# A fused transformer with a routed last layer: when the third slot's weights are loaded, how the experts are chosen, and where two norms stand

## The reference, cut to what matters

```python
x = x + _L0_xattn_ref(16, 64, 256, w, u, _layernorm(x), ctx)        # wkv, the first stage
...
x = x + _L2_ffn_ref(_layernorm(x), w_gate_up, w_proj)               # the ternary stage
x = x + _L3_xattn_ref(_layernorm(x), ctx, ctx)
x = x + _L3_ffn_ref(_layernorm(x), gate_w, w1, w2, w3)              # the experts:
    router_logits = x @ gate_w.T                                    # 1024 x 8
    probs = softmax(router_logits)
    top_w, top_i = top_k(probs, 2)
    top_w = top_w / sum(top_w)
    for e in range(8):
        h = silu(x @ w1[e].T) * (x @ w3[e].T)                       # 256 -> 896
        out = out + w_dense[:, e:e + 1] * (h @ w2[e].T)             # 896 -> 256
```

## Time and profile before

| | us |
|---|---|
| median of 3 runs | 753.79 (752.92 to 754.49) |
| the profiled execution | 752.44 |
| its span, first to last instruction | 750.7 |
| TensorE busy | 607.6 (81%) |
| VectorE busy | 463.6 (62%) |
| ScalarE busy | 304.8 (41%) |
| GpSimd busy | 235.4 (31%) |

### The profile page before, as it was taken

One profiled execution on the slowest core, in us unless ns is written; L12 is line 12 of the kernel. 1 busy time (PEld: TensorE's weight loads), 2 busy tenths in 40 slices (PEclk: granted clock), 3 DMA queues, 4 the chain that ended last, 5 costly groups with the idle time before them and its releaser, 6 DMA issues.

```text
span 750.7 us, 12278 instructions
## 1 busy us (share of the span) xinstructions
PE 607.6 (81%) x4701; PEld 458.9 (61%) x4701; DVE 463.6 (62%) x963; ACT 304.8 (41%) x512; POOL 235.4 (31%) x250
## 2 busy tenths in 40 slices
PE   1551999958841699999696998886999999999993
PEld 1241556736731255566443666546999999999993
DVE  6998688897889898997856777965111111111110
ACT  4920255436664158878643566611111111111110
POOL 3312065346401798620511312001122222222211
PEclk9875799989985589999997999989899999999998
DMA  8000502200025427550303000118599999899942
GB/s 281 0 0 0 183 5 69 68 4 2 2 47 127 100 56 182 159 137 31 114 1 148 1 1 1 56 59 338 204 316 321 324 310 323 302 330 320 314 138 70
DMA packets 39594, 102.14 MB, mean 136 GB/s; under 512 B 6648, under 2 KB 31096, under 8 KB 35256
## 3 DMA queue, kind: packets, MB, share of 16 engines
q1 hardware_dynamic: 29312, 89.69, 35.2%
q0 software_dynamic: 4368, 5.90, 3.9%
q10 hardware_dynamic: 5856, 5.77, 2.2%
HBM read 87.45 MB, written 14.55 MB: 136 GB/s over the span
## 4 chain that ended last, share of the span: by engine, by line
PE 56%; DVE 30%; issue 5%; ACT 3%; DMA 2%; POOL 2%; POOLq 0%; DVEq 0%; SPq 0%; ACTq 0%
PE bank L1935 19%; PE bank L1948 9%; PE bank L1497 5%; DVE region L1225 3%; PE bank L1098 3%; PE bank L1138 3%; PE bank L580 2%; DVE XN L375 2%; PE bank L1122 2%; PE bank L1517 2%; PE bank L514 2%; DVE region L2227 2%; PE bank L2058 2%; DVE region L784 1%; PE bank L2065 1%
## 5 line engine op out<-in xcount | busy, mean ns | idle before, releaser
L1935 PEld LDWEIGHTS bank<-wide,region 128*128 128x128 f32 x1288 | 149.4, 194 | 2.7 <-ACT wide L1852 1.6
L1935 PE MATMUL bank<-wide,region 128*128 128x128 f32 x1288 | 150.0, 277 | 1.0 <-ACT wide L1852 1.0
L1818 DVE TENSOR_TENSOR wide<-wide,bank 128x512 f32<-128x512 f32 (+1 forms) x46 | 28.6, 621 | 130.6 <-ACT wide L1862 130.6
L1862 ACT ACTIVATE wide<-bank 128x512 f32<-128x512 f32 (+1 forms) x46 | 25.0, 544 | 183.8 <-PE bank L1935 183.8
L1225 DVE TENSOR_REDUCE region<-bank 128x2 f32<-128x512 f32 x128 | 80.1, 680 | 6.9 <-PE bank L1098 6.3
L1948 PE MATMUL bank<-region,wide 128*128 128x256 f32 x322 | 73.4, 379 | 0.7 <-DVE wide L1829 0.7
L1161 ACT ACTIVATE region<-bank 128x1024 f32<-128x1024 f32 x64 | 62.9, 1024 | 15.7 <-PE bank L1122 15.5
L1702 POOL DMA_INDIRECT residual_rows<-wide,to_row x23 | 36.4, 1581 | 100.0 <-DMA residual_rows<-wide,to_row 77.3
L1948 PEld LDWEIGHTS bank<-region,wide 128*128 128x128 f32 x322 | 59.4, 190 | 8.2 <-issue 1.0
L1098 PE MATMUL bank<-region 128*128 128x256 bf16 x256 | 52.0, 305 | 8.9 <-DVE region L1225 5.8
L389 POOL TENSOR_TENSOR rstd<-vareps,half_neg 128x4 f32<-128x4 f32 x16 | 18.3, 1146 | 123.9 <-DVE vareps L385 123.9
(11 more groups left out here) (311 smaller groups left out, 1138.0 us busy)
## 6 DMA issues: line engine op xcount, KB each, us to landing
region<-in_L_ffn_experts_dram SPq DMA_DIRECT2D x23, 1792.0 KB, 9.6
region<-in_L_ffn_experts_dram SPq DMA_DIRECT2D x23, 896.0 KB, 4.8
region<-ctx_parts SPq DMA_DIRECT2D x24, 192.0 KB
region<-norm_parts SPq DMA_DIRECT2D x24, 192.0 KB
channel_values<-wide ACTq DMA_DIRECT2D x8, 512.0 KB, 4.4
ctx_parts<-region SPq DMA_DIRECT2D x40, 64.0 KB, 2.0
region<-in_L_ffn_w_gate_up_dram SPq DMA_DIRECT2D x4, 512.0 KB, 5.4
wide<-channel_values SPq DMA_DIRECT2D x16, 128.0 KB, 2.6
```

The source lines that it names most:

```text
L1818: e.tensor_tensor(HB8[par][:, cols], silu8[:, cols], bank[hf][:, 512:512 + P * (hi - lo)], ALU.mult)\
L1935: last = e.matmul(bank[hf][:, at_:at_ + P], w[:, col:col + P], xbT[par][:, P * c:P * c + P], start=(c == 0), stop=(c == KC - 1))
```

## The change

Six things change. (1) SP waits for slot 1's gathered rows before it loads slot 2's weights. (2) The two experts are chosen by the shifted logits, without the exponent; the probabilities and the weights of the two are made later, behind the row marks. (3) Slot 0's tokens are marked by their rank within expert 0 straight from the counts, ahead of the positions; the counts move to another bank, and fewer unused matmuls run. (4) `from_row` comes before `to_row`, and an unused lane gathers row 0, where it gathered the row with its own lane's number. (5) The lane weights' matmuls stand ahead of slot 2's transposes. `lo_hot` moves to another place in memory, and ScalarE and GpSimd each wait once for row numbers. (6) In the first stage the norm of tiles 0 to 3 stands behind GpSimd's loop; in the ternary stage the variance and normalisation of tiles 4 to 7 both come at step 1, behind the rest-of-rest subtraction.

```diff
             def second_half(t):
                 if t < 2:
                     vec_invert(e, 6 + t)
+
+            def rest_half(t):
                 if t == 1:
                     e.wait_ge(x_done, 5 * NT)
                     norm_variance(e, ch, 5, 4, NT)
-                if t == 2:
                     norm_tiles(e, 5, 4, NT)
...
-            tile_steps([(hidden, 0), (mean_square, 1), (rest, 1), (second_half, 0), (add, 2), (rest_of_rest, 1)], next_norm)
+            tile_steps([(hidden, 0), (mean_square, 1), (rest, 1), (second_half, 0), (add, 2), (rest_of_rest, 1), (rest_half, 0)], next_norm)
...
                 x8 = e.value_load(etab[0:1, s:s + 1], min_val=0, max_val=E8 - 1)
+                if s == 2:
+                    e.wait_ge(s_moe["rows_in1"], 16)
                 weights_in(e, s, L3_ffn_experts[bass.ds(x8, 1)].rearrange("x p w -> (x p) w"))
...
                     if s >= 1:
                         e.wait_ge(s_moe["hidden_ready"], 2 * s + hf - 1)
+                    elif hf == 1:
+                        e.wait_ge(s_moe["rows_known"], 1)
...
+            ch.link(e.iota(lane_below, [[1, P]], base=-N, channel_multiplier=0, allow_small_or_imprecise_dtypes=True))
...
-            e.wait_ge(s_moe["logits_exp"], 1)
-            ch.link(e.tensor_reduce(v["z"], r["ex"], AX.X, ALU.add))
-            ch.link(e.reciprocal(v["rz"], v["z"]))
-            ch.link(e.tensor_tensor(r["pr"], r["ex"], per_tile(v["rz"]), ALU.mult))
-            for src, m, o in (("pr", "m1", "o1"), ("p2", "m2", "o2")):
+            e.wait_ge(s_moe["logits_shifted"], 1)
+            for src, o in (("lg", "o1"), ("p2", "o2")):
+                if o == "o2":
...
+                else:
+                    ch.link(e.scalar_tensor_tensor(r["key"], r["lg"], 0.0, per_expert(rev8), ALU.is_equal, ALU.mult))
...
+            ch.link(e.tensor_tensor(nearest, ps(5, 0, NT), r["cnt"][:, 0, :], ALU.add))
+            ch.link(e.scalar_tensor_tensor(nearest, cnt_b[:, 0:NT], -float(N), nearest, ALU.mult, ALU.add))
+            for hf in range(2):
+                e.tensor_tensor(first_hot[:, 4 * hf:4 * hf + 4, :], lane_below.unsqueeze(1).broadcast_to([P, 4, P]),
+                                nearest[:, 4 * hf:4 * hf + 4].unsqueeze(2).broadcast_to([P, 4, P]), ALU.is_equal)\
+                    .then_inc(s_moe["first_marked"], 1)
...
-            ch.link(e.tensor_tensor(nearest, posk[:, 0, :], posk[:, 1, :], ALU.min))
-            for hf in range(2):
-                e.tensor_tensor(first_hot[:, 4 * hf:4 * hf + 4, :], lane_no.unsqueeze(1).broadcast_to([P, 4, P]),
-                                nearest[:, 4 * hf:4 * hf + 4].unsqueeze(2).broadcast_to([P, 4, P]), ALU.is_equal)\
-                    .then_inc(s_moe["first_marked"], 1)
...
-            e.wait_ge(s_moe["routing_made"], 3)
-            ch.link(e.tensor_copy(spare, ps(5, SLOTS, 2 * SLOTS)))
-            ch.link(e.scalar_tensor_tensor(source, ps(5, 0, SLOTS), -1.0, spare, ALU.add, ALU.add))
-            ch.link(e.scalar_tensor_tensor(spare, source, 0.0, spare_row, ALU.is_lt, ALU.mult))
-            ch.link(e.tensor_tensor(to_row[:, :], source, spare, ALU.add))
-            e.tensor_scalar(from_row[:, :], to_row[:, :], N - 1, None, ALU.bitwise_and).then_inc(s_moe["rows_known"], 1)
-
+            e.wait_ge(s_moe["logits_exp"], 1)
+            ch.link(e.tensor_reduce(v["z"], r["ex"], AX.X, ALU.add))
+            ch.link(e.reciprocal(v["rz"], v["z"]))
+            ch.link(e.tensor_tensor(r["pr"], r["ex"], per_tile(v["rz"]), ALU.mult))
+            for o, m in (("o1", "m1"), ("o2", "m2")):
+                ch.link(e.tensor_tensor(r["m"], r["pr"], r[o], ALU.mult))
+                ch.link(e.tensor_reduce(v[m], r["m"], AX.X, ALU.add))
             ch.link(e.tensor_tensor(v["den"], v["m1"], v["m2"], ALU.add))
             ch.link(e.reciprocal(v["den"], v["den"]))
             e.tensor_tensor(weight8[:, 0, :], v["m1"], v["den"], ALU.mult)
             ch.link(e.tensor_tensor(weight8[:, 1, :], v["m2"], v["den"], ALU.mult))
+
+            e.wait_ge(s_moe["routing_made"], 3)
+            ch.link(e.tensor_copy(spare, ps(5, SLOTS, 2 * SLOTS)))
+            ch.link(e.scalar_tensor_tensor(source, ps(5, 0, SLOTS), -1.0, spare, ALU.add, ALU.add))
+            e.tensor_scalar(from_row[:, :], source, 0.0, None, ALU.max).then_inc(s_moe["rows_known"], 1)
+            ch.link(e.scalar_tensor_tensor(spare, source, 0.0, spare_row, ALU.is_lt, ALU.mult))
+            e.tensor_tensor(to_row[:, :], source, spare, ALU.add).then_inc(s_moe["rows_known"], 1)
...
-            busy(4, 9)
+            busy(4, 5)
             e.wait_ge(s_moe["choices_made"], 1)
...
-            busy(4, 10)
+            busy(4, 3)
...
-                if s == 1:
+                if s == 2:
                     lane_weights()
...
                 e.tensor_tensor(EV[c][:, cols], E[c][:, cols], CT[:, c, cols], ALU.mult).then_inc(s_ev, 1)
-                if u == 2:
-                    pool_norm(e, 1, 0, 4)
+            pool_norm(e, 1, 0, 4)
             pool_norm(e, 1, 4, NT)
```

More of the change, by code:

```diff
@@ L306, in program @@
         chosen_at = small(2 * NT, E8)
-        rc = {n: small(NT) for n in ("mx", "z", "rz", "m1", "m2", "k", "den", "n", "nt", "end", "base", "least", "ones")}
+        rc = {n: small(NT) for n in ("mx", "z", "rz", "m1", "m2", "k", "den", "second", "nt", "end", "base", "least", "ones")}
         cnt_b = small(NT * E8 // 2).bitcast(BF16)
@@ L328, in program @@
         BLOCKS = ((0, 4), (4, I8 // P))
-        lo_hot = small(NT * P).bitcast(BF16).rearrange("p (j l) -> p j l", l=P)
         hi_hot = small(2 * NT * 2 * SLOTS // 2).bitcast(BF16).rearrange("p (j v s) -> p j v s", v=2, s=SLOTS)
@@ L334, in program @@
         weight_rest = carve(2, NT)
+        lo_hot = carve(2 * NT, P, dt=BF16)
         weight_part = [carve(2, NT, dt=BF16) for _ in range(3)]
-        lane_no, slot_no, tile_row = small(P), small(SLOTS), small(2 * NT)
+        lane_no, slot_no, tile_row, lane_below = small(P), small(SLOTS), small(2 * NT), small(P)
         slot_of, lane_of, posk = small(2, NT), small(2, NT), small(2, NT)
@@ L1698, in store @@
                 if s == 0:
+                    e.wait_ge(s_moe["rows_known"], 2)
                     e.wait_ge(s_moe["residual_stored"], 32)
@@ L1727, in vec_experts @@
             e.tensor_tensor(r["lg"], lg, per_tile(v["mx"]), ALU.subtract).then_inc(s_moe["logits_shifted"], 1)
-            e.wait_ge(s_moe["logits_exp"], 1)
-            ch.link(e.tensor_reduce(v["z"], r["ex"], AX.X, ALU.add))
-            ch.link(e.reciprocal(v["rz"], v["z"]))
-            ch.link(e.tensor_tensor(r["pr"], r["ex"], per_tile(v["rz"]), ALU.mult))
-            for src, m, o in (("pr", "m1", "o1"), ("p2", "m2", "o2")):
-                ch.link(e.tensor_reduce(v[m], r[src], AX.X, ALU.max))
-                ch.link(e.tensor_tensor(r["m"], r[src], per_tile(v[m]), ALU.is_equal))
-                ch.link(e.tensor_tensor(r["key"], r["m"], per_expert(rev8), ALU.mult))
+            e.wait_ge(s_moe["logits_shifted"], 1)
+            for src, o in (("lg", "o1"), ("p2", "o2")):
+                if o == "o2":
+                    ch.link(e.tensor_reduce(v["second"], r[src], AX.X, ALU.max))
+                    ch.link(e.tensor_tensor(r["m"], r[src], per_tile(v["second"]), ALU.is_equal))
+                    ch.link(e.tensor_tensor(r["key"], r["m"], per_expert(rev8), ALU.mult))
+                else:
+                    ch.link(e.scalar_tensor_tensor(r["key"], r["lg"], 0.0, per_expert(rev8), ALU.is_equal, ALU.mult))
                 ch.link(e.tensor_reduce(v["k"], r["key"], AX.X, ALU.max))
@@ L1739, in vec_experts @@
                 if o == "o1":
-                    ch.link(e.scalar_tensor_tensor(r["p2"], r["o1"], -2.0, r["pr"], ALU.mult, ALU.add))
+                    ch.link(e.scalar_tensor_tensor(r["p2"], r["o1"], NEG, r["lg"], ALU.mult, ALU.add))
             e.tensor_tensor(cnt_b.rearrange("p (e t) -> p t e", e=E8), r["o1"], r["o2"], ALU.add).then_inc(s_moe["choices_made"], 1)
@@ L1751, in vec_experts @@
             ch.link(e.tensor_tensor(v["base"], v["end"], v["nt"], ALU.subtract))
-            ch.link(e.tensor_tensor(r["pos"], ps(6, 0, 64).rearrange("p (e t) -> p t e", e=E8),
+            ch.link(e.tensor_tensor(r["pos"], ps(5, 0, 64).rearrange("p (e t) -> p t e", e=E8),
                                     r["cnt"].rearrange("p e t -> p t e"), ALU.add))
@@ L1885, in pe_experts @@
             last.then_inc(s_moe["routing_made"], 1)
-            busy(4, 9)
+            busy(4, 5)
             e.wait_ge(s_moe["choices_made"], 1)
-            e.matmul(ps(6, 0, 64), before, cnt_b, start=True, stop=True)
-            e.matmul(ps(6, 64, 128), onesb, cnt_b, start=True, stop=True).then_inc(s_moe["routing_made"], 1)
-            busy(4, 10)
+            e.matmul(ps(5, 0, 64), before, cnt_b, start=True, stop=True)
+            e.matmul(ps(5, 64, 128), onesb, cnt_b, start=True, stop=True).then_inc(s_moe["routing_made"], 1)
+            busy(4, 3)
```

4 lines of the change are left out of this document (2 added, 2 removed).

## The result

The changed kernel took 746.44 us (median of 4 executions, 746.21 to 748.16), the kernel before 754.14 beside it; the ratio is 0.9899 [0.9871, 0.9928], a gain of 7.6 us (here and below a gain is one less the ratio, times the median of before). Measured once more beside the later experiments it took 746.54 us against 755.39, ratio 0.9887 [0.986, 0.9915], a gain of 8.5. The forecast was 743.2 in 739.8 to 750.2: faster, as predicted, but 2 to 3 us short of the forecast gain of 10.6, and above the forecast's own bounds of 741 to 745.5; inside the range it lies because the range takes in the rivals. The profiled execution is the one of 748.16 us (span 746.4), so 4.3 us of span are to be found in it.

A forecast was written before the change was run, and what follows sets the result against it. The prediction took the chain of waits, 56% TensorE and 30% VectorE, as the bound; -3.2 (first stage) + 0.15 (ternary) - 7.55 (routing and slot 1) = -10.6 us gave 743.2 us, range 739.8 to 750.2.

The forecast's parts named there:

- First stage: Norm behind GpSimd's loop: the fourth unit's second scan no longer waits and ends 3.2 us earlier, carried to the end.
- Ternary stage: Moved subtraction fits VectorE's idle time, but VectorE waits for GpSimd's power: +0.15 us, bounds -0.3 and +1.1.
- Choices and marks: VectorE's routing chain: choices by logits save 1.54 us, marks by expert 0's ranks 1.81; slot 0's selection starts 3.35 earlier.
- Clock in the selection: Fewer fillers, so slot 0's row selection starts at 1.2 GHz: 2.0 us lost, between 0 and 3.
- Just in time: VectorE's marks and weight instructions end at 513.5 us, before the row tables at 514.0.
- Landing of slot 1's rows: With slot 2's weights held, the gather lands 2.9 us after issue, at 517.85 instead of 523.81: 5.95 us earlier.
- Slot 1's matmuls: TensorE pauses about 1 us instead of 5 and keeps 2.4 GHz: 6.25 us instead of 8.58, saving 2.33.
- the rival of the slow gather: Slot 1's gather still takes 7.1 us, as the first indirect DMA: total gain 4.1 us, 749.7 us; chance 0.16.
- Lane weights: Formerly inside TensorE's pause, they now stand between slot 1's matmuls and slot 2's transposes: +0.72 us.
- Weights of slots 2 on: Behind SP's new wait, slot 2's gate part still arrives with 5 us of slack; no cost, pitch 9.49 us.
- The rival of the empty lanes: Gathers of the last slots slow down as empty lanes all read row 0: 755.8 us at 175 ns a lane; chance 0.03.
- the rival by which the first stage's gain is taken up: Another engine in the following attention absorbs the first stage's 3.2 us: 746.4 us; chance 0.06.

The follow-up runs named there:

- e6_fillers: The changed kernel with nine and four filler matmuls ahead of the row selection instead of five and three: 747.99 us, ratio 0.9909.
- e3_routing: The changed kernel with both norm edits (first stage and ternary stage) undone, leaving the routing part alone: 749.96 us, ratio 0.992.
- e5_no_ternary: The changed kernel with its ternary-stage edit undone: 744.4 us, ratio 0.9852.
- e7_best: The changed kernel without the ternary edit, nine and four fillers, VectorE's weight instructions behind row numbers, hold moved to slot 1's down weights: 742.35 us, ratio 0.9824.
- e1_first_norm: The kernel before with only the first-stage edit (norm of tiles 0 to 3 behind GpSimd's loop): 751.42 us, ratio 0.9944.

## Why the prediction was right, and where it was off

- **First stage**, -3.2: measured -3.33 in the trace and -4.2 (2.6 to 5.8) in the time. Right, the norm beside the scan cost nothing, as taken.
- **Ternary stage**, +0.15: the step that failed. It said that "the subtraction (1.22) fits into the 1.65 us of idleness", and it does; but the idleness was a wait for GpSimd, and the subtraction slows the very work waited for. GpSimd's multiply goes from 0.73 to 1.58 us (1.59 once) in each of the six profiles with the edit. The row to price it from was there: the scan that took 2.27 us instead of 1.20 beside a GpSimd product, which the forecast used in the first stage alone. The other half of the term held (+0.26 against 0.15; the power fell from 2.01 to 1.02). At the transposes the trace thus gives +1.12; the times give +2.7 alone and +2.7 in the change. What lies between is, on the average of the fourteen profiles, the clock ahead of the logits: up to there the profiles with the edit are 2.2 us longer. Whether the edit brings the low clock there, or chance put it into five of six profiles against two of eight, stays open; with intervals of some 1.6 us either way, 1.1 is not excluded as the whole.
  The Trainium skill ("SBUF — State Buffer", Who interferes with whom) says that a VectorE instruction with two SBUF inputs contends with a GpSimd instruction that reads SBUF, that the ports they share are an exclusive lock, and that the order of issue decides who blocks. The trace agrees but for 0.15 us: VectorE's subtraction, which started first, ended at 393.96 + 1.17 = 395.13, and GpSimd's multiply 0.58 us later, at 395.71, though it takes 0.73 alone.
- **Choices and marks**, -3.35 for the selection's start: from the logits' end to the selection it is 507.11 - 501.71 = 5.40 us instead of 506.71 - 497.95 = 8.76, so -3.36.
- **Clock in the selection**, +2.0 (0 to 3): 5.26 us instead of 3.85, +1.4, and 4.70 to 4.84 in the other profiles with five and three fillers, so +0.9 to +1.0. But by `e6_fillers` the term isn't on the path. "Just in time" was right to a hair and a little worse: VectorE's weight instructions end at 517.14, with the row tables (516.73 + 0.41 = 517.14), so a clock that never falls gains nothing. The forecast says elsewhere that without this term the sum would be 2 us better; by its own figures (VectorE free at 513.5, the row tables at 514.0) it would have been 0.5.

The two rows on that tie, the timeline of the changed kernel's last weight instruction and of the first that makes row numbers, 0.09 us after it:

```profile
516.98 0.16 DVE L1796 TENSOR_TENSOR weight<-wide 128x8 f32<-128x8 f32 x1
517.23 0.18 DVE L1799 COPY wide<-bank 128x23 f32<-128x23 f32 x1
```

- **Landing of slot 1's rows**, -5.95: from the logits' end it is 521.24 - 501.71 = 19.53 us instead of 523.80 - 497.95 = 25.85, so -6.3. Right in mechanism and size (3.09 against 2.9 from the issue, and the issue 2.3 us earlier after the logits where 1.76 was forecast).
- **Slot 1's matmuls**, -2.33: -2.06 in the first profile, but -0.44 in the repeat and -0.43 in `e3_routing`, `e5_no_ternary` (both profiles) and `e6_fillers`. The forecast of "about 1 us" of pause was the condition, and it is nearly met in two of the seven profiles with the hold (1.39 and 1.19 us). This is the second term that was mis-sized. It would explain why the routing part measured -6.0 in the time, and not -7.55, though the interval (3.8 to 8.2) takes in both: from the logits' end to slot 1's down projection the profiles with the hold give 27.8 (the first), 29.45 (the repeat), 29.8 (`e3_routing`), 29.4 and 29.6 (`e5_no_ternary`), 29.9 (`e6_fillers`) and 26.5 (`e7_best`), against 533.81 - 497.95 = 35.86 before.
  In the time the hold is worth 3.7 to 4.6 us, where the rival of the slow gather stood 6.5 us apart (749.7 against 743.2); this fits slot 1's matmuls, which stay slow in most profiles with the hold too.
- **Lane weights**, +0.72: 0.54. **Weights of slots 2 on**, nothing: right, pitch 9.49.
- The rival of the empty lanes that all read row 0 has nothing for it: no gather DMA holds TensorE later on.

So each mechanism but one was right, that of slot 1's clock only in two profiles of seven. By the middles of the measurements, the 2 to 3 us that are missing are the ternary stage's 2.5 (2.7 less the 0.15 of the forecast) and about 1.5 of the routing (6.0 against 7.55), less the 1.0 that the first stage gave above its term; each of these has an interval of 1.6 to 2.2 us either way. One agreement is chance: the rival by which the first stage's gain is taken up gave 746.4, and 746.44 was measured, but `e1_first_norm` shows that this gain arrives.

## What to carry to other kernels

Before work is moved into an engine's idle time, look at what it waits for: if that is a GpSimd operation on SBUF and the moved work is a VectorE operation with two SBUF inputs, the wait itself can grow, and filling the gap can cost more than it saves (here 0.86 us at the statistics, where nothing was forecast). A small gather DMA that TensorE waits for can be worth holding back bulk loads for, even at the price of a wait in the loader's queue, as long as the ring behind it has slack (here some 4 us). Where a stretch of a few microseconds depends on the clock, forecast both levels with their chances; a single profile can't decide a term of 3 us, and neither can a single profile of the kernel before that it is compared with; an edit undone and timed can.

## What the runs showed of the hardware that was not expected

- The place of TensorE's low clock differs from run to run of one kernel: between 131 and 138 us the kernel before had 1.00 in one profile and 0.84 in the other, with 1.6 us lost between 98 and 138 us, and the same event in the middle of the program stood up to 4.5 us apart among nine profiles that have the same first stage.
- With fewer fillers the clock was lower where they had been, and once higher later: with more of them (`e6_fillers`) the selection runs at 2.4 GHz, TensorE finishes early, pauses 2.91 us, and slot 1's matmuls then take 8.15 us; with fewer, in the first profile, it pauses 1.39 us and they take 6.52. But in the repeat, with the same few fillers, it pauses 1.96 us and they take 8.14.
- Slot 1's gather DMA takes 2.96 to 3.57 us from its issue to its landing when the next 2.75 MB of weights are held back, and 6.99 to 7.16 when they are queued ahead of it, with nothing between in fourteen profiles.
